# Two bands at a time: copying and clearing PSUM banks in pairs while an adjacency matrix is built

## The reference, cut to what matters

```
dst = minimum(3125 * uniform(50000) ** 2.0, 99999)       # then everything is sorted by dst
# L0: five gated steps over the graph
messages = h[col] @ W_msg.T + b_msg                       # row = src, col = dst
agg = segment_sum(messages, row, num_segments=3125)
h = gru(agg, h)
x = layernorm(x + h)
# L1: three edge layers with gathers and segment sums, then a second layernorm
```

## Time and profile before

| | us |
|---|---|
| median of 3 runs | 2162.28 |
| runs | 2161.98 to 2163.98 |
| the profiled execution's own time | 2162.99 |
| its span | 2161.2 |
| first to last copy of a band (L752) | 62.7 to 272.1 |
| copies 196, clears L755 188, one each | 98.9 and 96.9 busy |
| TensorE, VectorE, ScalarE busy over the whole span | 1846.6, 1392.1, 651.3 |

### The profile page before, as it was taken

How to read it: one execution, slowest core, us unless ns; L and a number is a source line. 1 busy time by engine, 2 the same in 40 slices (tenths; PEclk the granted TensorE clock), 3 DMA queues, 4 the chain that set the end, 5 groups by cost and what they waited for, 6 DMA issues and landing times. The chain is left out here.

```text
span 2161.2 us, 47820 instructions
## 1 busy us (share of the span) xinstructions
PE 1846.6 (85%) x14213; PEld 1420.9 (66%) x14213; DVE 1392.1 (64%) x4633; ACT 651.3 (30%) x1281; POOL 982.8 (45%) x1025
## 2 busy tenths in 40 slices
PE   5777689999999995598888867999999879998995
PEld 2332244545444444488788747999999679998893
DVE  8998621313232326598888854777777558887785
ACT  1379811212121212233333332333333312111111
POOL 2000067710000000477777725777777267777770
PEclk7888889999999997799999988999999989999997
DMA  3145810030000004455455425777777345555551
GB/s 101 42 95 110 111 12 3 2 5 0 0 0 0 0 0 167 153 158 153 149 153 153 150 82 163 227 224 222 225 222 224 111 130 153 150 157 152 144 142 34
DMA packets 193826, 242.14 MB, mean 112 GB/s; under 512 B 56452, under 2 KB 120223, under 8 KB 192975
## 3 DMA queue, kind: packets, MB, share of 16 engines
q1 hardware_dynamic: 161199, 172.73, 28.7%
q0 software_dynamic: 31840, 57.21, 11.3%
q10 hardware_dynamic: 576, 9.44, 1.1%
HBM read 149.76 MB, written 69.88 MB: 102 GB/s over the span
## 5 line engine op out<-in xcount | busy, mean ns | idle before, releaser
L1601 POOL DMA_INDIRECT rows<-p_dram,src_i x864 | 830.9, 962 | 336.0 <-issue 239.9
L1839 DVE TENSOR_TENSOR agg_t<-psum,agg_t 128x128 f32 x1380 | 394.5, 286 | 158.9 <-PE psum L1718 135.8
L975 PE MATMUL psum<-adj,parts 128*128 (+2 forms) x1750 | 339.7, 351 | 5.9 <-ACT agg L1055 4.4
L1772 ACT ACTIVATE rows<-rows 128x512 f32<-128x512 f32 x216 | 136.2, 631 | 587.9 <-DVE rows L1832 576.8
L1823 DVE TENSOR_SCALAR hot_w<-col_f,dst_loc,weight 128x128 f32<-128x128 f32 x864 | 305.9, 359 | 0.8
L975 PEld LDWEIGHTS psum<-adj,parts 128*128 128x128 f16 x1750 | 153.0, 98 | 191.5 <-issue 23.4
L1698 PE MATMUL psum<-w_c,before 128*128 128x128 f32 x1840 | 261.4, 286 | 0.0
L1683 PE MATMUL psum<-p_sb,pair_src 128*128 x1032 | 153.1, 295 | 121.8 <-DVE pair_dst L1813 48.8
L923 DVE SCALAR_TENSOR_TENSOR gate_room<-psum,b_h,gate_room 128x512 f32<-128x512 f32 (+1 forms) x35 | 23.9, 683 | 348.2 <-ACT gate_room L1062 348.2
L840 POOL DMA_INDIRECT records<-record_of,place_i x128 | 125.2, 978 | 269.1 <-issue 269.1
L1718 PE MATMUL psum<-hot_w,rows 128*128 128x128 f32 x1728 | 233.7, 279 | 0.0
(11 more groups left out here) (251 smaller groups left out, 2375.2 us busy)
## 6 DMA issues: line engine op xcount, KB each, us to landing
e_dram<-after SPq DMA_DIRECT2D x230, 256.0 KB
before<-e_dram SPq DMA_DIRECT2D x230, 256.0 KB
adj<-stage SPq DMA_DIRECT2D x196, 97.8 KB, 3.9
pair_rows<-sorted_rows SPq DMA_DIRECT2D x129, 128.0 KB, 4.1
rows<-p_dram,src_i POOLq DMA_INDIRECT x864
hot_all<-dst_rows ACTq DMA_DIRECT2D x2, 3072.0 KB, 15.7
p_dram<-p_sb SPq DMA_DIRECT2D x6, 384.0 KB
records<-record_of,place_i POOLq DMA_INDIRECT x128, 2.1
```

Of the source, the lines that this page charges most:

```text
L975: mm = nc.tensor.matmul(psum[:, AGG_BANK, 0:n_cols], parts[:, w, part, :], adj[:, w, cols], start=(w == 0 and part == 0), stop=(w == WINDO ...
L1601: nc.gpsimd.indirect_dma_start(out=rows[:, b % ROWS, m * D:(m + 1) * D], out_offset=None, in_=p_dram, in_offset=bass.IndirectOffsetOnAxis( ...
L1772: nc.scalar.activation(e_of(q), source, ACT.Relu).then_inc(e_on, 1)
L1839: nc.vector.tensor_tensor(a, psum[:, A_BANKS[q % len(A_BANKS)], m * P:(m + 1) * P], a, ALU.add).then_inc(agg_on, 1)
```

## The change

ScalarE works on pairs of bands. The pairs are band 0 alone, then 1 and 2, 3 and 4, up to 193 and 194, and 195 alone, so that the two banks of a pair lie side by side. One copy takes both banks (128 x 782) to a stage tile of two bands. The stage has three such tiles, as many bytes as six single ones. One clear, of zeros repeated over two banks, follows the copy and waits for that same copy; before, a clear waited for the copy of the band before, and ran behind the next band's copy. The copy waits for the second band's last step, and for the landings of both transfers of three pairs earlier. The transfers themselves stay one a band, two of them now issued for each copy.

```diff
-        MOVES, BATCHES, STAGES, BANKS, AT_ONCE, PE_AT_ONCE, AT_A_TIME = 12, 3, 6, 8, 28, 28, 4
+        MOVES, BATCHES, STAGES, BANKS, AT_ONCE, PE_AT_ONCE, AT_A_TIME = 12, 3, 3, 8, 14, 28, 4
+        PAIRS = [range(max(g, 0), min(g + 2, BANDS)) for g in range(-1, BANDS, 2)]
-        stage = sb("stage", [P, STAGES, SPAN], F16)
+        stage = sb("stage", [P, STAGES, 2, SPAN], F16)
...
-                act.wait_ge(counted, ends[g % AT_ONCE] & 1023)
-                if g >= STAGES:
-                    act.wait_ge(laid[g % STAGES], 16 * (g // STAGES))
-                nc.scalar.copy(stage[:, g % STAGES, :], psum[:, (g + 1) % BANKS, 0:SPAN]).then_inc(staged, 1)
-                if 1 <= g <= BANDS - BANKS:
-                    act.wait_ge(staged, g)
-                    nc.scalar.copy(psum[:, g % BANKS, 0:SPAN], zeros[:]).then_inc(free, 1)
+                k, bank = len(pair), (pair[0] + 1) % BANKS
+                act.wait_ge(counted, ends[pair[-1] - first] & 1023)
+                if i >= STAGES:
+                    act.wait_ge(laid[i % STAGES], 16 * sum(len(PAIRS[j]) for j in range(i % STAGES, i, STAGES)))
+                nc.scalar.copy(stage[:, i % STAGES, 0:k, :], psum[:, bank:bank + k, 0:SPAN]).then_inc(staged, k)
+                if pair[-1] + BANKS < BANDS + 1:
+                    act.wait_ge(staged, pair[-1] + 1)
+                    nc.scalar.copy(psum[:, bank:bank + k, 0:SPAN],
+                                   zeros[:].unsqueeze(1).broadcast_to([P, k, SPAN])).then_inc(free, k)
...
+            for i, pair in enumerate(PAIRS):
+                for k, g in enumerate(pair):
+                    a = g % SPANS * BAND
+                    sp.wait_ge(staged, g + 1)
+                    sp.dma_start(adj[a:a + BAND, g // SPANS, :].rearrange("d (a b) -> d a b", a=SPANS),
+                                 stage[:, i % STAGES, k, :]).then_inc(laid[i % STAGES], 16)
```

More of the change, by code:

```diff
@@ L742, in _ @@
                 nc.scalar.copy(psum[:, (b + 1) % BANKS, 0:SPAN], zeros[:]).then_inc(free, 1)
-            for g in range(BANDS):
-                if g % AT_ONCE == 0:
+            for i, pair in enumerate(PAIRS):
+                if i % AT_ONCE == 0:
+                    first, behind = pair[0], PAIRS[min(i + AT_ONCE, len(PAIRS)) - 1][-1] + 1
                     _, ends = nc.values_load_multi_w_load_instructions(
-                        keep["band_end"][0:1, g:g + AT_ONCE], engines=(mybir.EngineType.Activation,),
-                        min_val=1, max_val=BAND_STEPS,
+                        keep["band_end"][0:1, first:behind], engines=(mybir.EngineType.Activation,), min_val=1, max_val=BAND_STEPS,
@@ L766, in _ @@
+            for j in range(STAGES):
+                sp.wait_ge(laid[j], 16 * sum(len(PAIRS[i]) for i in range(j, len(PAIRS), STAGES)))
             sp.wait_ge(zeroed, 2)
```

## The result

The changed kernel takes 2191.22 us (median of 4 runs, 2185.96 to 2193.11) against 2163.13 for the kernel before, run beside it: a ratio of 1.0128, 95% interval 1.0109 to 1.0147, or 28 us slower. The forecast was +2.8 us, in a range up to 2175. The profiled execution took 2189.72, its span is 2187.9.

What follows compares the result with a forecast made beforehand. TensorE's steps bound the stage until 203 us, then ScalarE (0.79 us a band) and transfers (0.81 to 0.94). Tail +1.4, before 203 us +0.8, end +0.6: +2.8 us, median 2162.28 to 2165.1, range 2158 to 2175.

Steps and rivals of the forecast that it cites:

- The step that failed: Tail: band ends still read once in 28 bands, most of each stall made good, 1 us left of 2.8.
- the tail: From band 119's copy at 203 us to band 195's: 76 bands at 0.91 us plus 1, 70.2 against 68.8, +1.4.
- behind the last copy: End of the stage: six copies without clears, copy and second issue later in pairs; +0.6 us, 0 to +1.5.
- The ring of stages: Stage tiles: a tile frees when both bands land, 1.45 us plus landing for three pairs; 0.91 us a band taken.
- the one before 203 us: From 150 to 203 us: ScalarE just keeps up, eight banks allow some lateness; +0.8 us, between 0 and +5.
- ScalarE's own time: Copy and clear of a pair: 1.56 us against 1.59 for two bands, 0.03 saved a pair.
- The transfers: Tail: if they limit at 107 to 113 GB/s, 0.89 to 0.94 us a band, landings settle at 3.9 to 4.2.
- The landings stay long: Slower rival: landings stay 4.5 to 4.8 us, ring at 0.99 to 1.04 a band, +12 to +18 us; chance 0.2.
- The ring doesn't bind: Faster rival: landings drop to 3.4 us, tail at 0.80 to 0.82 a band, 2156 to 2158 us; chance 0.15.
- nothing moves: Rival: gain and loss cancel, or transfers pace the tail at 0.87 either way; within 1.5 us of 2162.3; chance 0.2.
- The banks: TensorE's wait for cleared banks: `free` rising by two suits its groups of four steps; nothing either way.

Runs made afterwards that it cites:

- pair_aligned: The changed kernel with each reading of band ends started at its first pair's second band (0, 28, 56); 2170.65 us, 1.0039 of the kernel before.
- single_odd: The kernel before, single bands, with only the reading starts moved from multiples of 28 to 0, 27, 55 and so on; 2183.13 us, 1.0081.
- pair_behind: pair_aligned with the clear one pair behind, so it clears the banks of the pair before; 2171.85 us, 1.0051 of the kernel before.
- pair_act2_4: pair_aligned with four tiles, one reread column of zeros, and readings of four values once for two pairs; 2156.44 us, 0.9979 of the kernel before.
- pair_act2_4_behind: pair_act2_4 with the clear one pair behind; 2161.72 us, 1.0002 of the kernel before.
- single_act4: The kernel before, single bands, with ScalarE's readings of band ends cut from 28 values to 4; 2154.39 us, 0.9970 of the kernel before.
- single_mixed: The kernel before with readings started at bands 0, 28, 54, 81, 108, 136, 163, 190, some at multiples of 16 bytes; 2176.93 us, one run.

## Why the prediction was wrong

**The step that failed.** "The reading of band ends stays once in 28 bands; with the ring ahead of ScalarE's own 0.78, most of a stall is made good by the pairs after it, and I leave 1 us of the 2.8." The count is right but for one reading of a single value, the duration isn't: each of the six slow readings takes 6.4 us, not 2.0, and the stall is 5.8, not 1.4. Nor is it made good by the pairs after it: where the steps aren't the bound, each reading's whole difference stays in the end time. The start of the readings is 19 to 22 of the 28 us, shown by undoing it in the pairs (pair_aligned) and by doing it alone (single_odd). I had read this stall as a fixed price for 28 values from rows in which it was never longer than 1.6, and didn't look at what the diff did to the readings' start, nor ask the trace for their own line. No rival held it either. The kernel before has no reading with another start, so its trace could not have shown the factor of three; it did show a sequencer operation of 2 us that the change rewrote, and that deserved bounds of its own.

The sum had the stalls only in the tail, but four of the six slow readings lie before band 119, where the tail begins (203 us in the kernel before). The 28.4 us of the marker divide into +16.8 before the copy of band 119 (203.30 before, 220.13 after), where +0.8 was foretold, +12.2 in the tail (81.0 us from that copy to the last, foretold 70.2), and -0.7 behind the last copy, foretold +0.6. The copy that takes band 119, first after the change, then in pair_aligned:

```profile
220.13 0.81 ACT L754 CAST stage<-psum 128x782 f16<-128x782 f32 x1
```

```profile
207.58 0.81 ACT L754 CAST stage<-psum 128x782 f16<-128x782 f32 x1 [0.21 <-DMA adj<-stage]
```

**The ring of stages: mechanism right, size too small.** Total of the pairs' own cost: foretold +2.8, measured +8.4 by the ratio of pair_aligned and +6.3 by the marker. That the ring binds is shown by the landings and by the fourth tile; that it is the whole of the cost isn't. Its parts, from pair_aligned's rows: the copy of bands 119 and 120 starts at 207.58 where band 119's started at 203.30, so about 4 us were lost before 203 us, put at +0.8; from there to band 195 it takes 71.9 us, foretold 70.2, before 68.8; and behind the last copy it is 1 us shorter, not 0.6 longer. So the term mis-sized most is the one before 203 us, where I let the banks take the delay. Part of it may be the readings, 2.5 us for 27 values where they were 2.0 for 28; no run has short readings with three tiles.

**ScalarE's own time: wrong in sign.** Foretold 1.56 us a pair against 1.59. Copy and clear took 0.81, as worked out, but copy to clear 0.90, not 0.83, and clear to copy 0.75: 1.64 or 1.65 at best. The wait for its own copy costs 0.09 and not 0.03. What that is worth in the whole time stays open, for pair_behind also frees the banks later. The prediction also says that this trace doesn't bear out an overlap of 93 ns. A copy and a clear of 0.49 us each go in 0.79, so they overlap by about 0.1 each, and it roughly does; what differs is the duration, 0.49 us for 391 columns where the quoted formula gives 0.51.

**The transfers: half right.** I took 107 to 113 GB/s for what they can do, 0.89 us a band, and a DMA share of 1.10 to 1.16 for that of "most of this stretch". It is that of the three stretches of the earlier trace rows, 26 of 71 us. The other six between 203 and 256 us have 0.39 to 0.99, two of them:

```profile
225.00:234.00 9.00, 5.30 (x20) 1.96 (x20) 7.10 (x24) 9.00 (x24) 0.00 (x0) 0.95 0.58 116
...
252.00:256.00 4.00, 2.76 (x12) 1.06 (x11) 3.32 (x13) 4.00 (x11) 0.00 (x0) 1.00 0.99 126
```

So the trace of the kernel before had 126 GB/s already, and eight tiles gave that on the mean of 57 us. More under way gave a higher rate, but the number isn't all: pair_act2_4, with as many bytes of stage, has 116 GB/s from 203 to 260 us with a share of 0.99. The landings went the way foretold, to 3.6 us for the 4.0 I took.

**The rivals.** "The landings stay long" gave 2174 to 2181 by a mechanism that didn't occur: landings got shorter. "The ring doesn't bind" and "nothing moves" are out. **The banks** at nothing: no run tried them alone. In pair_behind and pair_act2_4_behind, where `free` comes a pair later, ScalarE's waits for steps grow by 11 to 12 us, so it isn't nothing.

## What to carry to other kernels

When a change regroups a loop, look at everything that is done once a group, the sequencer's readings of registers too: ask for their line, since neither busy groups nor waits name them, and "issue" in a wait is their mark. Keep such readings to multiples of 16 bytes and of four values; cut to four, ScalarE's readings were hidden behind its work here, but check each engine, for TensorE's weren't. And joining two items in a ring of the same bytes takes transfers from under way: price it as ring positions, not as bytes.

## What the runs showed of the hardware

- A register reading from SBUF took 1.85 to 2.3 us for 28 values from a multiple of 16 bytes, and 6.1 to 6.6 us for 27 or 28 from other starts. Four values took 0.31 us in single_act4 and 0.48 in pair_act2_4 (medians), one value 0.28 to 0.51. Four values an access, or one, at 0.22 to 0.28 us fits the rows of single_mixed.
- ScalarE goes from the end of a copy to a clear that waits for it in 0.09 us; without such a wait two operations of 782 columns overlap by 0.06 to 0.11.
- Transfers of 98 KB from one queue: 102 to 108 GB/s with three pairs of tiles, 114 to 116 with four (203 to 270 us); 120 with six single tiles and 126 with eight (203 to 260 us, short readings).
